# Second layer of a graph network on one core: the complex product across the edge in three real products, the radial matmuls in two row groups, the bias as bf16 parts

## What is computed

```python
R = relu(abs_distances[:, None] @ w1 + b1) @ w2 + b2      # 64 hidden units, 384 numbers for an edge
Y = spherical_harmonics(rel_vec)
Fj = features[src]                                        # 8 scalars and 8 vectors of 3
for i, (mo, lo) in enumerate(RS):                         # RS = [(8, 0), (8, 1)]
    for j, (mi, li) in enumerate(RS):
        for k, lf in enumerate(range(abs(lo - li), lo + li + 1)):
            C = _W3J[lo, lf, li]
            acc = acc + _NORM[i] * einsum('euv,ef,evi,ofi->euo', Rb[..., k], Yf, Fb, C)
out = zeros.at[dst].add(msg)
```

## Time and profile before

| | |
|---|---|
| median of 3 runs | 18546.1 us (18534.44 to 18557.52) |
| the profiled execution: its span | 20972.7 us |
| stage of the second layer in it | 6662 to 12475 us, 196 steps |
| mean granted TensorE clock | 0.732 of full speed |
| DVE over the span | 11202.5 us busy (53%), 19689 instructions |
| POOL over the span | 11778.5 us busy (56%), 10055 instructions |
| PE over the span | 13068.2 us busy (62%), 92471 matmuls |

### The profile page before, as it was taken

How to read it: one execution, slowest core, us unless ns; L and a number is a source line. 1 busy time by engine, 2 the same in 40 slices (tenths; PEclk the granted TensorE clock), 3 DMA queues, 4 the chain that set the end, 5 groups by cost and what they waited for, 6 DMA issues and landing times. The chain is left out here.

```text
span 20972.7 us, 293199 instructions
## 1 busy us (share of the span) xinstructions
PE 13068.2 (62%) x92471; PEld 7362.5 (35%) x92471; DVE 11202.5 (53%) x19689; ACT 3071.4 (15%) x5120; POOL 11778.5 (56%) x10055
## 2 busy tenths in 40 slices
PE   0565555555554676776766652555555555699999
PEld 0344434333333444444444431122222112355554
DVE  2565544444444777777777773333332222567777
ACT  0222222222221111111111110111111111000000
POOL 4788888888886555555555554666666665100000
PEclk6565555555556888888888885666666666799999
DMA  7333333333333222222222213333333343489998
GB/s 276 47 39 37 37 39 39 39 37 37 38 39 46 47 49 47 48 47 47 48 46 48 46 40 35 73 70 72 76 71 71 71 76 63 125 257 293 292 293 267
DMA packets 2998639, 1817.14 MB, mean 87 GB/s; under 512 B 1730466, under 2 KB 2755819, under 8 KB 2979019
## 3 DMA queue, kind: packets, MB, share of 16 engines
q1 hardware_dynamic: 2201756, 1336.87, 25.1%
q0 software_dynamic: 669312, 166.80, 11.3%
q10 hardware_dynamic: 126512, 300.38, 4.1%
HBM read 1474.43 MB, written 392.90 MB: 89 GB/s over the span
## 5 line engine op out<-in xcount | busy, mean ns | idle before, releaser
L2005 POOL DMA_INDIRECT xg<-d_tab,s_i x3136 | 3254.6, 1038 | 2615.5 <-POOLq L1996 1630.7
L2537 POOL DMA_INDIRECT xg<-d_tab,s_i x3136 | 2996.6, 956 | 1865.8 <-issue 954.8
L2265 PE MATMUL pR<-w,H 128*128 128x384 f32 x6272 | 2703.4, 560 | 1407.6 <-PEq L2259 834.5
L1403 POOL DMA_INDIRECT d_acc<-AG,ix x1568 | 2471.5, 1576 | 527.2 <-issue 459.5
L1403 POOL DMA_INDIRECT d_acc<-T,ix x1568 | 2466.3, 1573 | 478.3 <-issue 437.1
L2923 PE MATMUL pacc<-nodes,HB 128*32 128x512 fp8e4 x47040 | 2663.0, 380 | 42.7 <-PEq L2967 42.7
L2574 DVE TENSOR_TENSOR_SCAN U<-mU,U,up 128x512 f32<-128x512 f32 x392 | 501.6, 1280 | 3289.0 <-DVEq L2573 2688.6
L2265 PEld LDWEIGHTS pR<-w,H 128*128 128x128 f32 x6272 | 1225.8, 215 | 2533.1 <-issue 2182.8
L2695 PE MATMUL hb<-U,Wbc 128*128 128x512 f32 x784 | 642.4, 914 | 2204.7 <-PEq L2691 2023.1
L1756 PE MATMUL pm<-ms,eq 128*128 128x32 f32 x6272 | 1366.4, 399 | 890.5 <-PEq L1754 888.8
L2923 PEld LDWEIGHTS pacc<-nodes,HB 128*32 128x32 f16 x47040 | 1261.5, 97 | 1317.1 <-issue 57.1
(11 more groups left out here) (338 smaller groups left out, 17504.3 us busy)
## 6 DMA issues: line engine op xcount, KB each, us to landing
packed<-d_A SPq DMA_DIRECT2D x420, 1792.0 KB
row<-d_m SPq DMA_DIRECT2D x1568, 64.0 KB
xg<-d_tab,s_i POOLq DMA_INDIRECT x6272
wrow<-d_w SPq DMA_DIRECT2D x196, 512.0 KB
d_scan<-so ACTq DMA_DIRECT2D x392, 256.0 KB
d_A<-stage ACTq DMA_DIRECT2D x97, 784.0 KB
d_ea<-in_ea_t ACTq DMA_DIRECT2D x1, 50176.0 KB
d_exp<-T ACTq DMA_DIRECT2D x1, 50176.0 KB, 250.4
```

The costliest lines, as they stand in the source:

```text
L1403: e.indirect_dma_start(out=d_acc[i], out_offset=bass.IndirectOffsetOnAxis(ap=ix[k][:, t:t + 1], axis=0), in_=mo[k][:, t * F:(t + 1) * F], ...
L2005: e.indirect_dma_start(out=xg[k][:, t, :], out_offset=None, in_=d_tab, in_offset=bass.IndirectOffsetOnAxis(ap=s_i[n][:, t:t + 1], axis=0)) ...
L2265: last = e.matmul(pR[u % 2][:, j, 0:384], H[k][:, (2 * u + j) * P:(2 * u + j + 1) * P], w2[:, :], start=True, stop=True)
L2537: e.indirect_dma_start(out=xg[n][:, j * ST + c, :], out_offset=None, in_=d_tab, in_offset=bass.IndirectOffsetOnAxis(ap=s_i[d][:, col:col + ...
```

## The change

Three things change in the stage.

1. Across the edge, a*x - b*y and a*y + b*x are made from three products: (a + b) * (-y), a * (x + y) and (b - a) * x. The first two added give one component, the last two the other. The radial matmul gives 448 numbers instead of 384: 256 as before, then 8 inputs x 3 products x 8 outputs. DVE multiplies 192 of them per column instead of 2 x 128, and needs x + y first (line 2168 of the new kernel) and one addition of sums afterwards (line 2137), so `tail` has four parts. The products of `u` = 2 to 7 stand in memory as inputs, products, outputs, and are added over the inputs by a reduction of their own (line 2125).
2. The radial matmuls contract 64 hidden units instead of 65 rows padded to 128. One column uses partitions 0 to 63, the other 64 to 127, so a product `u` now holds columns `u` and `u + 8`. `H` is 128 x 1024 instead of 64 x 2048 elements.
3. The bias, which was row 65, is split into three bf16 parts and added by one bf16 matmul per column ahead of the fp32 one.

Smaller edits go with them: `PP` is split into `PPa` and `PPb`, ScalarE makes 4 copies in `spread` instead of 5 and 2 in `early_sums` instead of 1, and the loads of `wrow` and of the weights come in halves.

```diff
-            PP = sb(st, "PP", [P, 2, 2, 16, F])
-            Q = [sb(st, f"Q{k}", [P, 4, T, 8]) for k in range(2)]
+            PPa = sb(st, "PPa", [P, 2, 2, 8, 40])
+            PPb = sb(st, "PPb", [P, 2, 2, 8, 16])
+            Q = [sb(st, f"Q{k}", [P, 5, T, 8]) for k in range(2)]
...
                         if u < 2:
-                            to = PP[:, u, :, :, :]
-                            e.tensor_tensor(to[:, :, :, 0:16], pR[j][:, :, 0:256].rearrange("p t (r c) -> p t c r", c=16),
-                                            bc(FG[k][:, t, :], 3, 16), ALU.mult)
-                            for o in range(2):
-                                last = e.tensor_tensor(to[:, :, :, 16 + 8 * o:24 + 8 * o],
-                                                       pR[j][:, :, 256:384].rearrange("p t (u c) -> p t c u", c=16),
-                                                       bc(FX[k][:, t, o, :], 3, 8), ALU.mult)
-                            last.then_inc(S("PP"), 1)
+                            for of, c in ((PPa, 0), (PPb, 8)):
+                                last = e.tensor_tensor(of[:, u, :, :, 0:16],
+                                                       pR[j][:, :, 0:256].rearrange("p t (r c) -> p t c r", c=16)[:, :, c:c + 8, :],
+                                                       bc(FG[k][:, t, c:c + 8], 3, 16), ALU.mult)
+                            if u == 0:
+                                e.wait_ge(S("three"), 1)
+                                e.sem_inc(S("three"), -1)
+                            e.tensor_tensor(PPa[:, u, :, :, 16:40].rearrange("p t c (g u) -> p t c g u", g=3),
+                                            pR[j][:, :, 256:448].rearrange("p t (c g u) -> p t c g u", c=8, g=3),
+                                            bc(FX[k][:, u, :, :, :], 4, 8), ALU.mult).then_inc(S("PP"), 1)
                             return
...
-                        e.tensor_tensor(to[:, :, 16:32, :].rearrange("p t (o u) c -> p t o u c", o=2),
-                                        bc(pR[j][:, :, 256:384].rearrange("p t (u c) -> p t u c", c=16), 2, 2),
-                                        bc(FX[k][:, t, :, :], 3, 8), ALU.mult).then_inc(S(f"Pr{j}"), 1)
+                        e.tensor_tensor(to[:, :, 256:448].rearrange("p t (c g u) -> p t c g u", c=8, g=3),
+                                        pR[j][:, :, 256:448].rearrange("p t (c g u) -> p t c g u", c=8, g=3),
+                                        bc(FX[k][:, u, :, :, :], 4, 8), ALU.mult).then_inc(S(f"Pr{j}"), 1)
...
-                        e.tensor_reduce(Q[k][:, :, 2 * u:2 * u + 2, :].rearrange("p r t u -> p t r u"),
-                                        Pr[u % 3].rearrange("p t (r u) c -> p t r u c", u=8), axis=X, op=ALU.add
+                        e.tensor_reduce(Q[k][:, 0:2, u:T:8, :].rearrange("p r t u -> p t r u"),
+                                        Pr[u % 3][:, :, 0:256].rearrange("p t (r u c) -> p t r u c", u=8, c=16), axis=X, op=ALU.add)
+                        e.tensor_reduce(Q[k][:, 2:5, u:T:8, :].rearrange("p g t u -> p t g u"),
+                                        Pr[u % 3][:, :, 256:448].rearrange("p t (c g u) -> p t g u c", c=8, g=3), axis=X, op=ALU.add
                                         ).then_inc(S("vq"), 1)
...
+                            e.tensor_tensor(Q[k][:, 2:4, :, :], Q[k][:, 2:4, :, :], Q[k][:, 3:5, :, :], ALU.add
+                                            ).then_inc(S("pair"), 1)
...
+                        e.tensor_tensor(FX[k][:, :, :, :, 1], FX[k][:, :, :, :, 2], FX[k][:, :, :, :, 0], ALU.subtract
+                                        ).then_inc(S("three"), 1)
...
                                 sums(k, u - 1)
+                            if u == 3 and not first:
+                                tail((n + 3) % 4, 3)
...
                         for j in range(2):
-                            last = e.matmul(pR[u % 2][:, j, 0:384], H[k][:, (2 * u + j) * P:(2 * u + j + 1) * P], w2[:, :],
-                                            start=True, stop=True)
+                            half = slice(64 * j, 64 * j + 64)
+                            e.matmul(pR[u % 2][:, j, 0:448], onesr[half, :], b2s[half, :], start=True, stop=False)
+                        for j in range(2):
+                            half = slice(64 * j, 64 * j + 64)
+                            last = e.matmul(pR[u % 2][:, j, 0:448], H[k][half, u * P:(u + 1) * P], w2k[half, :],
+                                            start=False, stop=True)
```

More of the change, by code:

```diff
@@ L1900, in gnn_kernel @@
             e9 = [sb(st, f"e9{n}", [P, 3, T, 3]) for n in range(DEEP)]
-            wrow = [sb(st, f"wrow{n}", [64, GE]) for n in range(DEEP)]
-            H = [sb(st, f"H{k}", [P, GE]) for k in range(2)]
+            wrow = [sb(st, f"wrow{n}", [P, GE // 2]) for n in range(DEEP)]
+            H = [sb(st, f"H{k}", [P, GE // 2]) for k in range(2)]
             xg = [sb(st, f"xg{k}", [P, T, F]) for k in range(2)]
@@ L1964, in load @@
                                     d_fr[bass.ds(s + 4, 1), :, :].rearrange("a p x -> (a p) x")).then_inc(S(f"le{n}"), 16)
-                    for n in range(3):
-                        load(0, n, sources=False)
+                    load(0, 0, sources=False)
+                    load(0, 1, sources=False)
+                    e.wait_ge(S("bp"), 1)
+                    e.sem_inc(S("bp"), -1)
+                    for h in range(2):
+                        for i in range(3):
+                            row = 64 * h + i
+                            e.dma_start(b2s[row:row + 1, :], b2p[i][row:row + 1, :]).then_inc(S("lb"), 16)
+                    load(0, 2, sources=False)
                     with e.Fori(0, G // 4 - 1) as it:
@@ new lines, in _ @@
+                    e.wait_ge(S("vc"), 2)
+                    e.sem_inc(S("vc"), -2)
+                    for to, of in ((w2k, w2), (b2k, b2t[0])):
+                        pair = of[:, 256:384].rearrange("p (u d c) -> p d c u", u=8, d=2)
+                        three = to[:, 256:448].rearrange("p (c g u) -> p g c u", c=8, g=3)
+                        e.tensor_copy(to[:, 0:256], of[:, 0:256]).then_inc(S("vc"), 1)
+                        e.tensor_tensor(three[:, 0, :, :], pair[:, 0, :, :], pair[:, 1, :, :], ALU.add).then_inc(S("vc"), 1)
+                        e.tensor_copy(three[:, 1, :, :], pair[:, 0, :, :]).then_inc(S("vc"), 1)
+                        e.tensor_tensor(three[:, 2, :, :], pair[:, 1, :, :], pair[:, 0, :, :], ALU.subtract
+                                        ).then_inc(S("vc"), 1)
@@ L2028, in _ @@
+                    e.wait_ge(S("vc"), 8)
+                    e.sem_inc(S("vc"), -8)
+                    for i in range(3):
+                        e.tensor_copy(b2p[i][:, :], b2k[:, :]).then_inc(S("vc"), 1)
                         e.wait_ge(S("vc"), 1)
                         e.sem_inc(S("vc"), -1)
[L2030 to L2033, removed]
@@ L2152, in _ @@
                     sums(1, 7)
-                    e.wait_ge(S("qc"), 1)
-                    e.sem_inc(S("qc"), -1)
-                    for part in range(3):
+                    e.wait_ge(S("qc"), 2)
+                    e.sem_inc(S("qc"), -2)
+                    for part in range(4):
                         tail(3, part)
@@ L2270, in early_sums @@
                         for c in range(c0, c1):
-                            last = e.matmul(pQ[:, :, :], ident[:, :],
-                                            PP[:, :, :, c, :].rearrange("p u t r -> p (u t) r"), start=(c == 0), stop=(c == 15))
+                            of, r = (PPa, 40) if c < 8 else (PPb, 16)
+                            last = e.matmul(pQ[:, :, :, 0:r].rearrange("p u t r -> p (u t) r"), ident[:, :],
+                                            of[:, :, :, c % 8, :].rearrange("p u t r -> p (u t) r"), start=(c == 0), stop=(c == 15))
                         if c1 == 16:
```

115 lines of the change are left out of this document (68 added, 47 removed).

## The result

The changed kernel takes 19069.08 us (median of 4 runs, 19065.79 to 19076.55) against 18546.96 (4 runs, 18534.44 to 18557.52) of the kernel before on the same chip: 1.0283 times as long, 95% interval 1.0271 to 1.0295. It is slower by 522 us, 2.66 us for each of 196 steps. I had predicted slower, by 196 us, with a range up to 19010. The direction is right, the size is wrong by 327 us, 1.67 us a step.

What follows compares the result with a forecast made beforehand. DVE was taken as the bound, POOL close beside it. DVE 20.55 + reads 1.65 + wait 0.5 = 22.7 us a step against 21.7, +1.0 x 196 = +196 us, 18742 us; range 18400 to 19010.

Steps and rivals of the forecast that it cites:

- The step before: Stage step of the kernel before, put at 21.7 us: DVE's time and a little of POOL's, ends 21.5 and 23.7.
- The holds: DVE's long idle stretches in the first profile, taken to come from recording; their median is 2427 us under the profiled span.
- clean step: A profiled step without a hold, 21.53 us between running sums on DVE, taken as the stage's own rhythm.
- DVE's saving: DVE's products, reductions and two added instructions: together -0.98 us a step, to 20.55 us.
- The strided reads: Second reduction reading 384 numbers in steps of 24 words: +1.65 us a step, ends 0 and 2.7.
- full price: Rival: strided reads cost +2.7 us, 0.3 of the wait left, 18918 us; by the page's figure 19050 us. 17%.
- The wait behind `mg`: DVE waits for radial 5, queued on PE behind the transposes that need `mg`: 0.5 us a step.
- the time of before: PE's radial products: halfway between row groups one after the other (+0.6 us in the wait) and fully overlapped (-0.3).
- POOL sets the step: Rival: POOL's gather group, 22.5 us or more, hides DVE's 22.7: 0 to +40 us, 18546 to 18586. 21%.
- One after the other: Rival: PE's two row groups don't overlap, DVE waits several times a step: +160 to +350 us. 6%.

Runs made afterwards that it cites:

- e0: The kernel before, unchanged, profiled a second time: 18530.72 us.
- e11: The kernel before with every second gather left out, 8 of 16 a group: 18272.06 us, 0.9857 of before.
- e10: The changed kernel with the tail (tv and mg) back in its old places, strided reads kept: 18769.45 us, 1.0127 of before.
- e3: The changed kernel, second reduction reading in steps of 1, 2, 3, 8, 16 and 24 words for u = 2 to 7 (wrong numbers): 18729.36 us.
- e13: The changed kernel with only tv moved back between the products of u = 1 and 2: 18792.89 us, 1.0137 of before.
- e12: The changed kernel with both edge tiles of a radial product in the lower row group (wrong numbers): 20530.27 us, 1.1075 of before.
- e7: e2 with eight useless transposes in each of PE's two pauses a step: 18327.94 us, 0.9888 of before.
- e5: e2 with the tail (tv and mg) back in its old places: 18314.78 us, 0.9882 of before.
- e2: The changed kernel with the second product's columns reordered, so the reduction reads neighbours and computes the same sums: 18726.19 us, 1.01 of before.
- e4: e2 with the token for radial 1 given at the start of DVE's step: 18451.19 us, 0.9954 of before.
- e14: e2 with mg moved ahead of the sums of u = 2, tv left in place: 19395.51 us, 1.0461 of before.

## Why the prediction was wrong in size

- **The step before, 21.7 us.** Measured 22.81 (e0). The holds were not in the kernel's own time, as I took it: e0's profile has none and is as long as a run. But I chose DVE's clean step "and a little of POOL's" between the ends 21.5 and 23.7, and the steps I read as clean were those in which POOL, thanks to the holds elsewhere, had a lead (1067 us of waits for a free buffer, against 7.3 in e0). With POOL's load halved the step is 21.55 (e11). The error is 1.1 us, 218 us of the time, and it made the loss look larger than it is. Against 22.81 my own 22.7 for the changed kernel says no change: that the forecast had the right direction was luck.
- **DVE's saving, -0.98 us.** Right: e10's step is 24.01 us with 0.15 us of idleness left. Less six times (0.99 - 0.46) = 3.2 us for the reads (starts 9009.85 and 9010.84 above, 384 elements in neighbours 0.46), 20.7 remain; I had 20.55.
- **The strided reads, +1.65 us.** This term failed most: 3.2 us, above the high end of 2.7. My end was the rate of the running sum, 2.2 ns an element; the reduction takes (0.99 - 0.06) / 384 = 2.4. The middle between 0.26 ns at three words and that end had no row behind it, and the row that I held against the full price tells little of 24 words: e3 has 659 ns at 3 words and 1072 at 24. The Trainium skill's figure for 24 words (Vector Engine (DVE) Microarchitecture Reference, section "Measured stream behaviour on trn2"), 2.50 ns, was within 0.1 ns of this. The page states it for both sources or the output stepping; here one source does.
- **The wait behind `mg`, +0.5 us ahead of u = 5.** Wrong in place and size. Its own sum had a slip: 1.06, 1.06 and 0.27 are 2.39 us, not 2.3, so it gives 0.4. With the strided reads the wait at u = 5 is 0.11 us a step. Behind `mg`, which ends at 9011.38, radial 5 is done at 9013.82 and DVE asks for it at 9013.98; of these 2.6 us the strided reads of u = 3 are 0.53 more than with neighbours. I charged both terms in one sum, though the one hides the other. Of the 1.58 us that DVE does wait, 1.22 are ahead of u = 2. In my account of moved work I had asked what stands behind `mg`, not what `tv` had covered: it had stood between the products of u = 1 and u = 2 (e13: 276 of 300 us).
- **PE, "the time of before".** Work between tokens is shorter, 1.04 us a radial product against 1.30, the low end that I gave, since the row groups overlap almost fully (1.98 us in one group, e12). What I hadn't thought of is the rest of a quicker PE: 3.25 us in one place against 1.47. That both the shorter products and DVE's longer step lengthened it is read from the timelines, not tried apart. Its clock then falls to 0.50, and the next 4 us and more of its work, on DVE's path, take almost twice as long (e7).
- **The sum.** 20.7 + 3.2 + 1.6 = 25.5 us against 22.8 before. I had 22.7 against 21.7. The order of DVE's work undone gives back 300 us (e10), the reads undone as well 455 more (e5). DVE's own work is then 20.6 us a step, but POOL sets the step at 21.7, so that the saving of the three products shows in part at most: the kernel before was held by POOL as well, at 22.8, with DVE's work at 21.6.
- **The rivals.** "Full price" had the right mechanism and was short of it; by the page's figure it gave 19050 us, near the 19069 measured, but only because the errors of its other terms cancel (the step before -1.1 us, the wait 0.3 instead of 1.6), which is luck too. "POOL sets the step" was right of the kernel before and wrong of the one after. "One after the other" is excluded by e12.

## What to carry to other kernels

When the profile at hand has holds, take no clean step as the step of the kernel until another engine's waits are ruled out in it; profile again if possible. When work moves along an engine's queue, ask of the place that it leaves what it covered there, not only what it delays where it goes. And when PE becomes faster than the engine that feeds it tokens, look at the granted clock behind its pauses. Here three remedies helped on e2: other work of DVE across the slow stretch (e5, 411 us), the pause filled (e7, 398 us) and the token brought forward (e4, 275 us).

## What was not expected of the hardware

- Steps of two words are as cheap as neighbours in a reduction (545 and 546 ns for 384 numbers), and the price doesn't grow evenly: 16 words (783) are cheaper than 8 (831). The views differ in their number of loops too, which the runs don't separate.
- The low clock doesn't follow every pause. In e14 one of 2.46 us was followed by it and one of 2.27 us, 16 us later, was not: the windows from 9019 on show 1.00. In e12 PE was at 0.50 for the 13 us from 9000 on while busy all the time; ahead of a like stretch (9031.88) it had rested 1.39 us. What decides is open.
- Radial products in two row groups of 64 rows run almost fully beside each other, in fp32 too: 1.04 us for both with their bias, 1.98 in one group.
